# Row loads of the column scatters: asked for by GpSimd in the middle of each step, in place of SP's queue

## The chip, the core and the metric

The program runs on 1 core of one Trainium2 chip. Engines: PE is TensorE (matmuls), PEld its weight loads, DVE is VectorE, ACT is ScalarE, POOL is GpSimd, SP is SyncE, which here only asks for transfers. Each engine works through its own instructions in program order and waits for others by semaphores. The metric is the time of one execution in device microseconds; the median of three runs before the change is 14245.91 us (14245.34 to 14246.84).

## The reference, cut to what matters

The program is a tower of eight blocks on 128 images of 64 x 64. The first is a Fourier neural operator of four layers; then come attention and expert layers, and at the end a graph attention over 8192 nodes with 262144 listed edges and one loop per node, 270336 in all, followed by experts. What the change touches serves that graph block:

```python
loops = jnp.arange(M, dtype=edge_index.dtype)
src = jnp.concatenate([edge_index[0], loops])
dst = jnp.concatenate([edge_index[1], loops])
...
e_max = jax.ops.segment_max(e, dst, num_segments=M)
ee = jnp.exp(e - e_max[dst])
denom = jax.ops.segment_sum(ee, dst, num_segments=M)
...
agg = jax.ops.segment_sum(msg, dst, num_segments=M).reshape(M, HEADS * NUM_EXPERTS) + b_gat
```

The kernel computes these segment operations on edges sorted by `dst`. It sorts in two passes (a radix sort): first by the low 7 bits of the node ("column"), then by the rest ("row"). The first pass and the ranks of the second run beside the Fourier block.

## The kernel before, in words

`fno` is one stage between two barriers of all engines (`Tower.stage`, barriers at L59 and L65). It works through 16 units (4 groups of 32 images x 4 layers), each of 4 chunks of 8 images, so 64 chunks, numbered n = 0 to 63. In a chunk PE makes eight products `to_y` (L566), counted by the semaphore `y_done` (512 in all), each followed by the product with `f_proj` (L547) that is summed in a bank for `f_qa`. DVE adds that sum to `f_qa` once a chunk (L762, `q_added`), and the first L547 of the next chunk waits for that add. ACT moves and rectifies between the products. At the end of a unit comes the blend (L590), at the end of a group the head (L597), whose result `hq` is written out by `h_out` (L400, to `tower_h`); the first L652 of the next group waits until that has landed.

Beside it runs the column pass of the sort:

- DVE ranks the edges, a few columns per chunk (`rank_part`, before the chunk's L762). The 2112 columns of 128 edges are ranked in 4 parts of 528; `placed` counts parts that are ready.
- POOL scatters them: 48 steps of 44 columns, one indirect DMA per column (L2097), 128 rows of 8 bytes to `sorted1` at places `r_pos`. Step k begins when `y_done` has reached `send_at(k) + 1` (96 + 5.5 k, rounded down, plus 1) and its second half of 22 columns at `send_at(k) + 4`. The scatters of step k count on semaphore k mod 8 (`pool_column0` to `pool_column7`).
- Its source rows are loaded into one of two halves of `r_rows` by `rows(k)` (L375 to L378), 44 KB each. `rows(k)` waits until all scatters of step k - 2 have landed.
- At chunk 50 (`ROW_CHUNK`) the sorted list is read back: SP loads the `nodes` in four parts (L390) after `scattered`, DVE takes the row keys from them (L2091) and counts them (L2073) in chunks 50 to 52, and ranks them in the chunks from 53 on.

The order of SP's queue is written out in `sync` (L402 to L434): per unit the weights of the next (`f_stage`, L368), then chunk by chunk what is due there, then `projection_in` (`f_proj`, L373) and, after a group's last unit, `h_out`. `group_in` (L361 to L363) loads the next group's image, spectrum and features at chunk 2 of a group's last unit. `rows(k + 2)` stands at chunk (send_at(k) + 4) // 8.

Of the kernel before, what the change touches and what calls it, by code (L numbers as in the profile page):

```python
# [195 lines left out]
HD_SENDS = 8  # L196
# [111 lines left out]
def fno(t, d, ranks):  # L308
# [4 lines left out]
    send_at = lambda k: FIRST_SEND + 11 * k // 2  # L313
# [4 lines left out]
    with ExitStack() as ctx:  # L318
# [27 lines left out]
        with t.stage(*names) as (block, g_loaded, x0_done, x0_moved, x1_done, x1_moved, lift_done, lift_moved, q0_done, q0_moved,  # L346
                                 staged, wm_ready, proj_in, x_done, x_moved, t_done, t_moved, a_done, a_moved, y_done, r_done, used, q_added,
                                 f_moved, e_done, e_moved, w_done, spec_added, own, relu_done, o_done, o_moved, h_sent, rows_even, rows_odd, counted, summed, based, placed, place_out, scattered, nodes_in, nodes_used, row_placed, row_out, *sent):
            rows_in = (rows_even, rows_odd)
# [6 lines left out]
            @block.sync  # L356
            def _(sp):
                def group_in(gi):
                    if gi >= 1:
                        sp.wait_ge(a_done, 32 * LAYERS * gi)  # L360
                    sp.dma_start(xi, d["image_y"][gi].rearrange("y b x -> y (b x)")).then_inc(g_loaded, 16)  # L361
                    sp.dma_start(x16, d["grid_spectrum"]).then_inc(g_loaded, 16)
                    sp.dma_start(feat, d["features"][gi]).then_inc(g_loaded, 16)  # L363

                def weights_in(u):
                    if u >= 1:
                        sp.wait_ge(wm_ready, 6 * u)
                    sp.dma_start(stage[:].rearrange("p a b c e -> p (a b c e)"), f.folded[u % LAYERS]).then_inc(staged, 16)  # L368

                def projection_in(u):  # L370
                    if u >= 1:
                        sp.wait_ge(used, yi(u, 0, 0))
                    sp.dma_start(proj[:].rearrange("p c o y -> p (c o y)"), f.projections[u % LAYERS]).then_inc(proj_in, 16)  # L373

                def rows(k):  # L375
                    if k >= 2:
                        sp.wait_ge(sent[(k - 2) % HD_SENDS], 16 * STEP_COLS * ((k - 2) // HD_SENDS + 1))
                    sp.dma_start(ranks.rows[:, k % 2], ranks.edges[:, k * STEP_COLS:(k + 1) * STEP_COLS, :]).then_inc(rows_in[k % 2], 16)  # L378

                def place_part(part):  # L380
                    sp.wait_ge(placed, part + 1)
                    sp.dma_start(ranks.column_place[:, part * QC:(part + 1) * QC], ranks.pos[:, part]).then_inc(place_out, 16)

                def nodes(part):
                    if part == 0:
                        sp.wait_ge(scattered, 1)
                        sp.wait_ge(place_out, 16 * PARTS)
                    else:
                        sp.wait_ge(nodes_used, part)
                    sp.dma_start(ranks.nodes[:], ranks.by_column[:, part * QC:(part + 1) * QC, :]).then_inc(nodes_in, 16)  # L390

                def row_part(part):
                    sp.wait_ge(row_placed, part + 1)
                    if part == 0:
                        sp.dma_start(ranks.end, ranks.ends[0:1, :]).then_inc(row_out, 16)
                    sp.dma_start(ranks.row_place[:, part * QC:(part + 1) * QC], ranks.pos[:, part]).then_inc(row_out, 16)

                def h_out(gi):
                    sp.wait_ge(o_moved, 2 * (gi + 1))
                    sp.dma_start(f.h[:, gi * PAIRS:(gi + 1) * PAIRS, :], hq).then_inc(h_sent, 16)  # L400

                group_in(0)  # L402
                weights_in(0)
                projection_in(0)
                rows(0)
                rows(1)
                for u in range(UNITS):
                    if u + 1 < UNITS:
                        weights_in(u + 1)
                    for ch in range(CHUNKS):  # L410
                        n = u * CHUNKS + ch
                        if ch == 2 and last_of(u) and u + 1 < UNITS:
                            group_in(u // LAYERS + 1)
                        for k in range(SEND_STEPS - 2):
                            if (send_at(k) + 4) // 8 == n:
                                rows(k + 2)
                                if k % PART_STEPS == 1:
                                    place_part(k // PART_STEPS)
                        if n == ROW_CHUNK:
                            for part in range(PARTS):  # L420
                                nodes(part)
                        if n > ROW_CHUNK:
                            for part in range(PARTS):
                                if row_done_at(part) == n - 1:
                                    row_part(part)
                    if u + 1 < UNITS:
                        projection_in(u + 1)
                    if last_of(u):
                        h_out(u // LAYERS)
                sp.wait_ge(h_sent, 16 * IGROUPS)  # L430
                for part in range(PARTS):
                    if row_done_at(part) >= UNITS * CHUNKS - 1:
                        row_part(part)
                sp.wait_ge(row_out, 16 * (PARTS + 1))  # L434

            @block.gpsimd
            def _(p):
                for k in range(SEND_STEPS):
                    p.wait_ge(placed, k // PART_STEPS + 1)
                    p.wait_ge(rows_in[k % 2], 16 * (k // 2 + 1))  # L440
                    p.wait_ge(y_done, send_at(k) + 1)
                    ranks.send(p, k, 0, STEP_COLS // 2, sent[k % HD_SENDS])
                    p.wait_ge(y_done, send_at(k) + 4)
                    ranks.send(p, k, STEP_COLS // 2, STEP_COLS, sent[k % HD_SENDS])
                for j in range(HD_SENDS):
                    p.wait_ge(sent[j], 16 * STEP_COLS * SEND_STEPS // HD_SENDS)
                p.sem_inc(scattered, 1)
# [1572 lines left out]
PARTS = 4  # L2020
QC = COLS // PARTS
STEP_COLS = 44
PART_STEPS = QC // STEP_COLS
SEND_STEPS = PARTS * PART_STEPS
# [476 lines left out]
def rows(v):  # L2501

    return np.tile(v[None], (P, 1))
# [153 lines left out]
```

## Time and profile before

| | |
|---|---|
| median of the runs | 14245.91 us |
| profiled execution, its own time | 14248.64 us |
| its span | 14246.8 us |
| granted TensorE clock, mean | 0.716 |
| PE busy | 8506.4 us (60%) |
| DVE busy | 6583.8 us (46%) |
| ACT busy | 3350.6 us (24%) |
| POOL busy | 6318.2 us (44%) |
| scatters of L2097 | 2112, 2049.9 us, mean 971 ns |

The profile is of one execution, in microseconds from the span's start. "Busy" is the time in which an engine worked; waits are put down to what released the engine, by semaphore events, and "issue" is time for which the profile shows no releaser. A row of the SP timeline with "x3" merges three issues and the time between them. A time in brackets at the end of a row is the engine's idle time before it. The Fourier stage lies between about 144 and 5256 us.

### The profile page before, as it was taken

The numbers are of one execution on the slowest core, as the hardware profiler recorded it, in microseconds if no ns is written. First come the engines' busy times: TensorE is split into PE (matmuls) and PEld (weight loads), VectorE is DVE, ScalarE is ACT, GpSimd is POOL, SyncE is SP. The second block draws the span as 40 slices with busy tenths as digits, with TensorE's granted clock in tenths as the row PEclk, the third lists the DMA queues.
The fourth block names the chain that finished last, engine by engine and source line by source line (L and its number), as shares of the span: only waits on it lengthen the run. The fifth ranks groups of instructions, "written<-read, shape, count | busy, mean of one in ns | idle before, by whom it ended". The sixth has DMA issues, their size and how long they took to land. (4 is left out here: it accounts for less than half of the span.)

```text
span 14246.8 us, 157338 instructions
## 1 busy us (share of the span) xinstructions
PE 8506.4 (60%) x62435; PEld 5418.0 (38%) x62435; DVE 6583.8 (46%) x9074; ACT 3350.6 (24%) x5899; POOL 6318.2 (44%) x6565
## 2 busy tenths in 40 slices
PE   6997798588899967987777774749520000000006
PEld 4775575366667735652222222536310000000004
DVE  5778376200007862139999994452421111111123
ACT  2443343244344432222222221222100000000001
POOL 0005577767710002646666663000036666666640
PEclk8997888788989875559999996555555555555555
DMA  2000000000000000000000001000001111111100
GB/s 102 9 11 18 12 12 11 19 12 20 11 25 9 12 18 10 1 1 2 2 2 2 2 2 1 1 0 0 0 10 19 19 19 17 19 19 19 17 12 7
DMA packets 290069, 178.08 MB, mean 12 GB/s; under 512 B 226797, under 2 KB 274957, under 8 KB 284752
## 3 DMA queue, kind: packets, MB, share of 16 engines
q0 software_dynamic: 209952, 32.71, 3.9%
q1 hardware_dynamic: 79472, 136.16, 3.0%
q8 instruction: 480, 7.86, 0.2%
q14 instruction: 165, 1.35, 0.0%
HBM read 116.87 MB, written 51.56 MB: 12 GB/s over the span
## 5 line engine op out<-in xcount | busy, mean ns | idle before, releaser
L2010 POOL DMA_INDIRECT sorted<-by_row_rows,by_row_idx x2112 | 2031.1, 962 | 2650.9 <-PE bank L1219 1729.1
L2097 POOL DMA_INDIRECT sorted<-r_rows,r_pos x2112 | 2049.9, 971 | 1926.3 <-PE bank L566 1284.5
L2229 POOL DMA_INDIRECT g_g<-table,g_idx x2112 | 2024.7, 959 | 643.6 <-issue 643.6
L1722 DVE TENSOR_TENSOR a_top<-bank,a_k 128x2048 f32<-128x2048 f32 x1024 | 2254.0, 2278 | 6.3 <-ACT a_k L1758 3.8
L2331 PE MATMUL bank<-sc_ident,g_tails 128*20 128x128 f32 x99 | 18.2, 307 | 3136.7 <-PEq L65 3134.9
L1884 PE MATMUL bank<-a_top,sc_pick_row 128*32 128x512 f32 x8192 | 1105.0, 620 | 515.5 <-DVE a_top L1722 492.6
L2331 PEld LDWEIGHTS bank<-sc_ident,g_tails 128*20 128x20 f32 x99 | 7.1, 98 | 3147.6 <-issue 3135.0
L2250 DVE CAST g_nodef<-g_es 128x64 f32<-128x64 int32 x33 | 6.4, 195 | 2492.9 <-DMA g_ep<-sorted 2492.9
L762 DVE TENSOR_TENSOR f_qa<-f_qa,bank 128x512 f32<-128x512 f32 x128 | 82.2, 684 | 2318.6 <-PE bank L556 1982.7
L547 PE MATMUL bank<-f_space,f_proj 128*128 128x512 f32 x2048 | 978.5, 601 | 199.7 <-issue 160.5
L1219 PEld LDWEIGHTS bank<-sw_e_w,e_hid 128*128 128x128 f32 (+1 forms) x4608 | 893.1, 329 | 363.6 <-issue 293.4
L2086 DVE TENSOR_TENSOR_SCAN r_run<-r_hit,r_base 128x528 f32<-128x528 bf16 x772 | 1017.3, 1318 | 27.6
L2227 POOL DMA_INDIRECT g_g<-table,g_first x33 | 31.1, 941 | 2139.2 <-DVEq L57 1741.8
L566 PE MATMUL bank<-f_space,f_to_y 96*128 96x512 f32 x2048 | 966.5, 599 | 19.1 <-ACT f_space L666 19.1
L1219 PE MATMUL bank<-sw_e_w,e_hid 128*128 128x64 f32 (+1 forms) x4608 | 933.9, 421 | 2.2 <-DVE e_part L1334 2.2
L681 ACT ACTIVATE f_space<-bank,f_b1r 128x512 f32<-128x512 f32 x1024 | 647.5, 683 | 832.8 <-PE bank L566 832.8
L556 PEld LDWEIGHTS bank<-f_from_y,f_space 128*128 128x128 f32 x6144 | 750.1, 193 | 185.4 <-issue 185.4
L556 PE MATMUL bank<-f_from_y,f_space 128*128 128x96 f32 x6144 | 741.0, 274 | 0.0
L1334 DVE TENSOR_TENSOR e_part<-bank,e_gates 128x512 f32<-128x512 f32 (+1 forms) x288 | 161.9, 571 | 1243.5 <-PE bank L1219 1243.4
L506 PE MATMUL bank<-f_space,f_spec 32*32 32x128 f32 x18432 | 521.9, 338 | 276.7 <-ACT f_space L652 211.7
L547 PEld LDWEIGHTS bank<-f_space,f_proj 128*128 128x128 f32 x2048 | 388.2, 192 | 675.2 <-issue 639.3
L1884 PEld LDWEIGHTS bank<-a_top,sc_pick_row 128*32 128x32 f32 x8192 | 166.8, 109 | 1228.1 <-DVE a_top L1722 1184.0
(467 smaller groups left out, 13013.8 us busy)
## 6 DMA issues: line engine op xcount, KB each, us to landing
f_stage<-folded SPq DMA_DIRECT2D x16, 2304.0 KB
sorted<-r_rows,r_pos POOLq DMA_INDIRECT x2112, 2.1
sorted<-by_row_rows,by_row_idx POOLq DMA_INDIRECT x2112, 2.1
g_g<-table,g_idx POOLq DMA_INDIRECT x2112, 2.6
states<-g_st SPq DMA_DIRECT2D x33, 768.0 KB
fp_raw<-t_modes SPq DMA_DIRECT2D x4, 2304.0 KB, 15.0
folded<-fp_turned SPq DMA_DIRECT2D x4, 2304.0 KB, 7.8
f_bb<-t_features SPq DMA_DIRECT2D x4, 2048.0 KB, 11.4
```

The source lines that it names most:

```text
L506: last = pe.matmul(out, spec[rows, kg, kx, r, :], rhs, start=(r == 0), stop=(r == 1), skip_group_check=True)
L547: last = pe.matmul(t.bank[4 + hf][:, :], proj[:, cg].rearrange("p o y -> p (o y)"), rr[:, cg % 2 * 2 + hf, :], start=(cg == 0), stop=(cg = ...
L556: last = pe.matmul(t.bank[6 + cg % 2][:, b * 96:(b + 1) * 96], rr[:, cg % 2 * 2 + hf, b * P:(b + 1) * P], const["from_y"][:, hf * 96:(hf + ...
L566: last = pe.matmul(t.bank[cg % 2 * 2 + hf][:, :], const["to_y"][:, hf * P:(hf + 1) * P], aa[:, cg, :], start=True, stop=True)
L681: last = act.activation(rr[:, cg % 2 * 2 + hf, :], t.bank[cg % 2 * 2 + hf][:, :], ACT.Relu, bias=f.b1r[:, u % LAYERS, cg:cg + 1])
L1219: last = pe.matmul(y_of(n, q)[:, col:col + D], hid[r, (2 * n + a) % HR, k * P:(k + 1) * P], w2[r, 2 * s + a, :], start=(j == 0), stop=(j = ...
L1722: v.tensor_tensor(top[:, n % RD].rearrange("p q (h s) -> p q h s", s=S), q, kk, ALU.max).then_inc(top_done, 1)
L1884: last = pe.matmul(sums[k % 2][32 * q:32 * q + 32, :], t.pick_row[:, i, :], top[:, n % RD, q, :], start=False, stop=(i == I16 - 1), skip_g ...
L2010: p.indirect_dma_start(out=self.dst, out_offset=bass.IndirectOffsetOnAxis(ap=self.idx[:, k:k + 1], axis=0), in_=self.rows[:, k, :], in_off ...
L2086: c.link(v.tensor_tensor_scan(self.run[:], self.hit[:], self.hit[:], self.base[:, i:i + 1], ALU.add, ALU.bypass))
L2097: p.indirect_dma_start(out=self.dst, out_offset=bass.IndirectOffsetOnAxis(ap=self.pos[:, k // PART_STEPS, at:at + 1], axis=0), in_=self.ro ...
L2229: p.indirect_dma_start(out=g[:, k_in, j, :], out_offset=None, in_=d["table"], in_offset=bass.IndirectOffsetOnAxis(ap=idx[:, k_in, j:j + 1] ...
```

## The change

The row loads leave SP's queue and are asked for by POOL. `rows(0)` stands at the start of POOL's part of the stage; `rows(k + 1)` stands in the middle of step k, between its two halves of 22 scatters, and waits for the scatters of step k - 1. `place_part` stays in SP at the same chunks. Nothing else changes.

```diff
--- before.py
+++ after.py
@@ -372,11 +372,6 @@
                         sp.wait_ge(used, yi(u, 0, 0))
                     sp.dma_start(proj[:].rearrange("p c o y -> p (c o y)"), f.projections[u % LAYERS]).then_inc(proj_in, 16)
 
-                def rows(k):
-                    if k >= 2:
-                        sp.wait_ge(sent[(k - 2) % HD_SENDS], 16 * STEP_COLS * ((k - 2) // HD_SENDS + 1))
-                    sp.dma_start(ranks.rows[:, k % 2], ranks.edges[:, k * STEP_COLS:(k + 1) * STEP_COLS, :]).then_inc(rows_in[k % 2], 16)
-
                 def place_part(part):
                     sp.wait_ge(placed, part + 1)
                     sp.dma_start(ranks.column_place[:, part * QC:(part + 1) * QC], ranks.pos[:, part]).then_inc(place_out, 16)
@@ -402,8 +397,6 @@
                 group_in(0)
                 weights_in(0)
                 projection_in(0)
-                rows(0)
-                rows(1)
                 for u in range(UNITS):
                     if u + 1 < UNITS:
                         weights_in(u + 1)
@@ -411,11 +404,9 @@
                         n = u * CHUNKS + ch
                         if ch == 2 and last_of(u) and u + 1 < UNITS:
                             group_in(u // LAYERS + 1)
-                        for k in range(SEND_STEPS - 2):
-                            if (send_at(k) + 4) // 8 == n:
-                                rows(k + 2)
-                                if k % PART_STEPS == 1:
-                                    place_part(k // PART_STEPS)
+                        for part in range(PARTS):
+                            if (send_at(PART_STEPS * part + 1) + 4) // 8 == n:
+                                place_part(part)
                         if n == ROW_CHUNK:
                             for part in range(PARTS):
                                 nodes(part)
@@ -435,11 +426,19 @@
 
             @block.gpsimd
             def _(p):
+                def rows(k):
+                    if k >= 2:
+                        p.wait_ge(sent[(k - 2) % HD_SENDS], 16 * STEP_COLS * ((k - 2) // HD_SENDS + 1))
+                    p.dma_start(ranks.rows[:, k % 2], ranks.edges[:, k * STEP_COLS:(k + 1) * STEP_COLS, :]).then_inc(rows_in[k % 2], 16)
+
+                rows(0)
                 for k in range(SEND_STEPS):
                     p.wait_ge(placed, k // PART_STEPS + 1)
                     p.wait_ge(rows_in[k % 2], 16 * (k // 2 + 1))
                     p.wait_ge(y_done, send_at(k) + 1)
                     ranks.send(p, k, 0, STEP_COLS // 2, sent[k % HD_SENDS])
+                    if k + 1 < SEND_STEPS:
+                        rows(k + 1)
                     p.wait_ge(y_done, send_at(k) + 4)
                     ranks.send(p, k, STEP_COLS // 2, STEP_COLS, sent[k % HD_SENDS])
                 for j in range(HD_SENDS):
```

In SP's queue around the end of the first group (unit 3), before. `f_bb` is a group's image and features, `f_stage` the next unit's weights, `pool_column`n the semaphores of the scatters, `used` and `wm_ready` PE's and ACT's progress:

```order
L368 DMA f_stage<-folded 128x4608 [waits wm_ready]
L378 DMA r_rows<-listed 128x88 [waits pool_column0]
L378 DMA r_rows<-listed 128x88 [waits pool_column1]
L382 DMA place<-r_pos 128x528 [waits placed]
L378 DMA r_rows<-listed 128x88 [waits pool_column2]
L361 DMA f_bb<-t_image_y 64x2048 [waits a_done]
L362 DMA f_space<-t_grid_spectrum 16x4608
L363 DMA f_bb<-t_features 128x4096
L378 DMA r_rows<-listed 128x88 [waits pool_column3]
L378 DMA r_rows<-listed 128x88 [waits pool_column4]
L378 DMA r_rows<-listed 128x88 [waits pool_column5]
L373 DMA f_proj<-projections 128x1024 [waits used]
```

The same place in SP's queue now (line numbers have moved: `h_out`, L400 before, is L395):

```order
L368 DMA f_stage<-folded 128x4608 [waits wm_ready]
L377 DMA place<-r_pos 128x528 [waits placed]
L361 DMA f_bb<-t_image_y 64x2048 [waits a_done]
L362 DMA f_space<-t_grid_spectrum 16x4608
L363 DMA f_bb<-t_features 128x4096
L373 DMA f_proj<-projections 128x1024 [waits used]
L395 DMA tower_h<-f_space 128x1024 [waits o_moved]
```

Six row loads, each with a wait for scatters, no longer stand between the weights' load and the projection's.

POOL's queue from the stage's start, before:

```order
L2097 DMA sorted<-r_rows,r_pos 270336x2 [waits y_done,rows_even,placed]
L2097 DMA sorted<-r_rows,r_pos 270336x2 x21
L2097 DMA sorted<-r_rows,r_pos 270336x2 [waits y_done]
L2097 DMA sorted<-r_rows,r_pos 270336x2 x21
L2097 DMA sorted<-r_rows,r_pos 270336x2 [waits y_done,rows_odd,placed]
```

The same place now (L2096 is the scatter, L432 the row load):

```order
L432 DMA r_rows<-listed 128x88
L2096 DMA sorted<-r_rows,r_pos 270336x2 [waits y_done,rows_even,placed]
L2096 DMA sorted<-r_rows,r_pos 270336x2 x21
L432 DMA r_rows<-listed 128x88
L2096 DMA sorted<-r_rows,r_pos 270336x2 [waits y_done]
L2096 DMA sorted<-r_rows,r_pos 270336x2 x21
L2096 DMA sorted<-r_rows,r_pos 270336x2 [waits y_done,rows_odd,placed]
L2096 DMA sorted<-r_rows,r_pos 270336x2 x21
L432 DMA r_rows<-listed 128x88 [waits pool_column0]
L2096 DMA sorted<-r_rows,r_pos 270336x2 [waits y_done]
```

One row load stands between the two halves of each step, and from the second step on it waits for the scatters of the step before.

## Rows read from the trace of the kernel before

**Rows 1.** The page, busy tenths of the span in 40 slices, TensorE and GpSimd.
```profile
PE   6997798588899967987777774749520000000006
...
POOL 0005577767710002646666663000036666666640
```

**Rows 2.** Timeline of PE: start us, length us, operation, [idle before].
```profile
5293.77 3.63 PE L826 MATMUL bank<-sc_ident,a_x 128*64 128x128 f32 x16 [48.42 <-PEq L65]
```

**Rows 3.** Waits of SP, 0 to 4200: releaser, total us, times, longest.
```profile
SPq L378 <- DMA sorted<-r_rows,r_pos: 2735.2, 46, 126.2
```

**Rows 4.** Timeline of the SP queue, 1300 to 4100.
```profile
1323.27 0.47 SPq L361 DMA_DIRECT2D f_bb<-t_image_y  x1
...
1379.88 111.61 SPq L378 DMA_DIRECT2D r_rows<-listed  x3
1491.54 0.43 SPq L373 DMA_DIRECT2D f_proj<-projections  x1
1492.01 0.43 SPq L400 DMA_DIRECT2D tower_h<-f_space  x1
...
2191.81 0.43 SPq L373 DMA_DIRECT2D f_proj<-projections  x1
...
4003.61 0.33 SPq L373 DMA_DIRECT2D f_proj<-projections  x1
...
4081.91 0.32 SPq L368 DMA_DIRECT2D f_stage<-folded  x1
```

**Rows 5.** Waits of PE, 1100 to 5300.
```profile
PE bank L506 <- ACT f_space L652: 211.7, 2, 106.5
PE bank L547 <- issue: 160.5, 5, 50.4
...
PE bank L456 <- DMA f_bb<-t_features: 32.4, 2, 19.1
```

**Rows 6.** Waits of ACT, 1100 to 5300.
```profile
ACT f_space L652 <- DMA tower_h<-f_space: 214.1, 2, 107.7
```

**Rows 7.** Timeline of PE at two of its stalls.
```profile
1498.31 5.36 PE L506 MATMUL bank<-f_space,f_spec 32*32 32x128 f32 x144 [106.50 <-ACT f_space L652]
...
2195.58 3.75 PE L547 MATMUL bank<-f_space,f_proj 128*128 128x512 f32 x4 [50.41 <-issue]
```

**Rows 8.** Line L373 (loads of f_proj): issue to landing.
```profile
DMA to landing us min/median/max: 3.4/3.7/17.2
```

**Rows 9.** Timeline of DVE: adds to f_qa and the first row key.
```profile
2237.14 1.28 DVE L762 TENSOR_TENSOR f_qa<-f_qa,bank 128x512 f32<-128x512 f32 x2 [79.61 <-PE bank L556]
...
4242.60 0.43 DVE L2091 TENSOR_SCALAR r_run<-r_nodes 128x528 int32<-128x528 int32 x1
...
4307.19 1.29 DVE L762 TENSOR_TENSOR f_qa<-f_qa,bank 128x512 f32<-128x512 f32 x2
...
4357.51 1.29 DVE L762 TENSOR_TENSOR f_qa<-f_qa,bank 128x512 f32<-128x512 f32 x2
```

**Rows 10.** Timeline of POOL: its two waits between first and last scatter.
```profile
1566.43 0.96 POOL L2097 DMA_INDIRECT sorted<-r_rows,r_pos  x1 [76.42 <-PE bank L566]
...
2949.46 0.95 POOL L2097 DMA_INDIRECT sorted<-r_rows,r_pos  x1 [56.46 <-PE bank L566]
```

**Rows 11.** Line L2097 (scatters): duration ns, first and last start us, landing.
```profile
L2097 POOL DMA_INDIRECT sorted<-r_rows,r_pos x2112: 952/958/1654, 1150.9 to 3975.7; - x192
...
DMA to landing us min/median/max: 2.1/2.1/6.5
```

**Rows 12.** Line L378 (row loads in SP): issue ns min/median/max.
```profile
L378 SPq DMA_DIRECT2D r_rows<-listed x48: 319/320/433, 146.8 to 3866.8; - x48
```

**Rows 13.** Line L390 (loads of the nodes): issue to landing.
```profile
DMA to landing us min/median/max: 3.6/3.9/10.6
```

**Rows 14.** Groups of POOL in 3000 to 3900 and in 2250 to 2500.
```profile
L2097 POOL DMA_INDIRECT sorted<-r_rows,r_pos x713 | 682.7, 957 | 217.4 <-issue 216.5 <-PE bank L566 0.9
...
L2097 POOL DMA_INDIRECT sorted<-r_rows,r_pos x194 | 191.5, 987 | 59.1 <-issue 59.1
```

## The prediction, made before the changed kernel ran

> **What bounds the kernel now.** I began with the busy slices [rows 1]. GpSimd (POOL) works in slices 4 to 12, the Fourier stage of the program, where TensorE (PE) is at eight or nine tenths in most slices but falls to seven and five in some. So PE sets this stage's pace and is held up somewhere. After the stage all engines meet at a barrier: PE's first work behind it waits for L65, the barrier's line [rows 2]. A microsecond saved ahead of the barrier is therefore a microsecond of the whole, and the question is only what ends this stage.
>
> SP's own waits come next [rows 3]. The row loads of L378 waited 2735.2 us on earlier scatters, in 46 instalments of up to 126.2 us. SP is one queue in program order, so all that stands behind such a wait is late too. The SP timeline shows which transfers those are [rows 4]: the image of the next group at 1323.27, which stood behind a row load that had just come free; `f_proj` at 1491.54 and `tower_h` at 1492.01, straight behind three row loads spread over 111.61 us; `f_proj` again at 2191.81, and so at three later places. Where no row load stands ahead (4003.61), `f_proj` goes out by itself.
>
> Does anybody wait for these? ACT waited 214.1 us in two places for `tower_h` to land [rows 6], and of PE's waits [rows 5] 211.7 us are for what ACT wrote then (L652), 160.5 us in 5 places stand at L547 and are put down to "issue", and 32.4 us in 2 places are for `f_bb<-t_features`. L547 is the product with `f_proj`: at 2195.58 PE has stood idle for 50.41 us and starts 3.8 us after SP's issue of 2191.81 [rows 7, 4], which is the landing time of `f_proj` (median 3.7 us) [rows 8]. These three rows are PE time lost to SP's row loads: 211.7 + 160.5 + 32.4 = 404.6 us, all before chunk 50, where the sorted list is first read.
>
> **What the change does to it, term by term.** SP loses 48 transfers and their 46 waits. `place_part` stays, but waits for a part that VectorE (DVE) has long finished. The loads that PE and ACT missed then go out when their own condition is met, as at 4003.61. I count the whole 404.6 us as gone from PE's chain up to chunk 50. DVE should not take PE's place there: its ranking is the same, and it waited 79.61 us for PE before the add at 2237.14 [rows 9]; with PE 50.41 us sooner [rows 7] some 29 us of wait are left.
>
> DVE begins the row keys of chunk 50 at 4242.60 [rows 9], right behind the add of chunk 49, for which it waits on PE. By PE alone that would become 4242.6 - 404.6 = 3838.0.
>
> But the row keys also need the scatters finished. POOL runs from 1150.9 to 3976.7 (last start 3975.7 and 0.96 for it) [rows 11]. In between it waited twice for PE's L566, 76.42 and 56.46 us [rows 10]. Both come behind stalls of PE that go: at 1566.43 PE is at least the 106.50 us of 1498.31 [rows 7] sooner, at 2949.46 more. So 132.9 us go, and the 2112 scatters end at 3976.7 - 132.9 = 3843.8, about the earliest possible, since nothing but 0.30 us stands between one scatter and the next.
>
> Into this chain the change puts 47 row loads (the 48th, `rows(0)`, is at the stage's start, where POOL is idle until 1150.9). No plain DMA asked for by POOL is in this trace. The near rows: SP's issue of the same load takes 0.320 us [rows 12], POOL's scatter 0.958 us, at most 1.654 us [rows 11], each plus 0.30 us between. Low end: 0.62 us each, 29 us. High end: 1.95 us each, 92 us. I take POOL's own scatter, also 128 partitions with a small piece each: 0.97 + 0.30 = 1.27 us, and 47 x 1.27 = 60 us. The new wait of each load, for the scatters of the step before, costs nothing: they were asked for at least 22 x 1.27 = 28 us earlier and land in 2.1 us, at most 6.5 [rows 11]. What is queued behind the load on POOL is 22 scatters, so the rows have the same 28 us to land before POOL asks for them.
>
> POOL then ends at 3843.8 + 59.7 = 3903.5. The last scatter lands (2.1 us); SP, which by then stands at `nodes(0)`, since the `f_stage` load ahead of it (4081.91 before [rows 4]) is past by 3677, issues (0.32) and the nodes land (3.9 [rows 13]): 3903.5 + 6.3 = 3909.8. That is 72 us later than PE would allow, so POOL becomes the bound, and the row keys start 4242.6 - 3909.8 = 332.8 us sooner than before.
>
> The rest of the unit shifts by the same. From the first row key to the add of chunk 50 DVE needs 64.6 us (4242.60 to 4307.19), and to that of chunk 51 another 50.3 us (4357.51), with no wait for PE ahead of either [rows 9]. PE, now ahead, stops at its first L547 of chunk 51 until the add of chunk 50 is done and is held by DVE to the unit's end, so its next work also starts 333 us sooner. From there all is as before.
>
> Sum against the profiled execution: 14248.64 - 332.8 = 13915.8. The median of the runs, 14245.91, lies 2.7 below that execution, which gives **13913 us**, 2.3% less.
>
> **Two pages of the Trainium skill against the rows.** Its page "DMA: Bandwidth & Descriptors", section "Issuing engines are not separate DMA queues", says that spreading DMAs over issuing engines saves only the time of issuing them, usually small. By that rule 48 x 0.32 us of SP would be all that is saved, and no time. The trace speaks against it here, since what SP's queue holds back is not the issuing but the waits in front of it (2735.2 us [rows 3]); its result is the second rival. The page "SBUF — State Buffer", section "SBUF: two separate sides", warns that a DMA issued from GpSimd stands still while VectorE holds the port that the two share, and gives some 620 ns alone against some 3100 ns beside such a copy. By it, 47 loads at 3.1 + 0.3 us would be an estimated 160 us. The rows show little of it: the same scatter takes a mean of 957 ns while DVE hardly works (3000 to 3900) and 987 ns while it ranks (2250 to 2500) [rows 14].
>
> **Rivals.** First, a dear row load. If POOL spends over 2 us on each plain load, the gain shrinks by 47 us for each microsecond. Against it: the 2112 scatters on this engine all stay under 1.66 us. For it: no such load is in the trace. At 4 us each: 3843.8 + 188 + 6.3 = 4038, a gain of 204.5 us, 14041 us.
>
> Second, no change. If PE's 160.5 us at L547, named only as "issue", and ACT's 214.1 us had other causes than SP's order, PE would still reach chunk 50 at 4242. POOL's 60 us would lie inside its 4242.6 - (3976.7 + 6.3) = 260 us of slack there, and the time is 14246. Against it: the stall ends 3.8 us behind SP's issue.
>
> Third, slower. One mechanism: POOL's chain grows past the point at which chunk 50 waited for PE. It decides from (4242.6 - 3843.8 - 6.3) / 47 = 8.35 us per load on, be it by issue or because the rows land so late in POOL's own queue, behind 22 scatters, that POOL waits for them (landing after 28 + 7 us). At 10 us each the row keys start at 4320, 77 us late: 14323 us. Against it: scatters land in 2.1 us at the median, so the queue is not backed up.
>
> **How the numbers follow.** Forecast (loads of 0.6 to 2 us, POOL the new bound) 0.80, dear load 0.12, no change 0.03, slower 0.05. Within the first the ends are 13913 - 31 = 13882 and 13913 + 32 = 13945. The range goes up to 13990, a load of 2.9 us, and starts at 13878. The runs shown differ by 0.01%; 0.2% (28 us) is taken as what a measurement tells from no change. Faster by that needs a load under 7.8 us: 0.92; same 0.03; slower 0.05.
>
> **What would show it.** In the profile of the changed kernel: no wait of SP for scatters; ACT without the 214.1 us for `tower_h`; L547 without idle times of 30 to 50 us; POOL without idle time for L566 after its first scatter, its last scatter near 3903; 48 plain loads on POOL of about 1 us; and as a new wait some 72 us of DVE's row keys for `r_nodes`, with PE held at L547 of chunk 51. It would be wrong if the last scatter came before 3870 or after 3950, if POOL waited for its rows, if DVE held PE in chunks 16 to 31, or if the stage ended earlier by another figure than POOL's.

## The result

The changed kernel takes 13885.71 us (median of 4 runs, 13873.11 to 13896.99) against 14246.38 us before (4 runs): a ratio of 0.9746, 95% interval 0.9729 to 0.9763. The forecast was 13913 (range 13878 to 13990). The profiled execution took 13896.99 us, its span is 13895.2 us.

SP's waits in the profile after, the line that answers [rows 3] being gone (columns: releaser, total us, times, longest):

```profile
SPq L373 <- PE bank L555: 2047.3, 9, 269.8
SPq L361 <- PE bank L529: 512.2, 3, 171.7
...
SPq L395 <- ACT f_space L700: 265.9, 4, 192.1
SPq L385 <- POOLq L446: 202.6, 1, 202.6
```

No row load waits for scatters in SP's queue any more. The one wait of SP for POOL that is left is that of the nodes (L385) for the end of all scatters: SP stood there for 202.6 us before POOL was through. Every load now waits for its own condition only, as the SP timeline shows (against [rows 4]): `f_bb` goes out at 1254.37 in place of 1323.27 and `tower_h` (now L395) at 1323.96 in place of 1492.01.

```profile
1254.37 0.47 SPq L361 DMA_DIRECT2D f_bb<-t_image_y  x1
...
1323.96 0.33 SPq L395 DMA_DIRECT2D tower_h<-f_space  x1
...
3885.09 15.18 SPq L385 DMA_DIRECT2D r_nodes<-sorted  x4
```

PE's waits (against [rows 5]: 211.7, 160.5 and 32.4 us, all gone), and what stands there now:

```profile
PE bank L546 <- DVE f_qa L761: 84.1, 5, 45.2
...
PE bank L596 <- ACT f_qa L697: 61.2, 4, 30.1
```

ACT has no wait for `tower_h` any more ([rows 6] had 214.1 us). POOL's waits in the same stretch: none of the two of [rows 10], only the 1005.6 us ahead of the first scatter and 1.5 us in five places, each of them the 0.30 us that stand between any two scatters.

```profile
POOL sorted L2096 <- PE bank L565: 1007.1, 6, 1005.6
POOL sorted L2096 <- issue: 642.0, 2106, 0.3
```

POOL's scatters and its row loads by line (duration ns min/median/max, first and last start; against [rows 11, 12]):

```profile
L2096 POOL DMA_INDIRECT sorted<-r_rows,r_pos x2112: 954/958/1937, 1151.2 to 3882.8; - x192
```

```profile
L432 POOL DMA_DIRECT2D r_rows<-listed x48: 570/582/704, 144.9 to 3799.9; - x48
```

The last scatter ends at 3882.8 + 0.96 = 3883.8. SP asks for the nodes at 3885.09 and DVE's first row key starts at 3888.76 (against 4242.60 in [rows 9]), after a wait that was not there before:

```profile
3888.76 0.43 DVE L2090 TENSOR_SCALAR r_run<-r_nodes 128x528 int32<-128x528 int32 x1 [47.58 <-DMA r_nodes<-sorted]
...
3894.34 0.44 DVE L2090 TENSOR_SCALAR r_run<-r_nodes 128x528 int32<-128x528 int32 x1 [4.68 <-DMA r_nodes<-sorted]
```

PE, ahead by then, is held at the first L546 of chunk 51, as forecast, and the stage ends (PE's first work behind the barrier, against 5293.77 in [rows 2]) at 4940.15:

```profile
3955.25 3.75 PE L546 MATMUL bank<-f_space,f_proj 128*128 128x512 f32 x4 [45.21 <-DVE f_qa L761]
```

```profile
4940.15 3.63 PE L825 MATMUL bank<-sc_ident,a_x 128*64 128x128 f32 x16 [48.26 <-PEq L65]
```

So the row keys start 353.8 us sooner, the stage ends 353.6 us sooner, and the profiled execution is 351.65 us shorter (14248.64 - 13896.99); 2.0 us are given back behind the stage.

The four runs lie in two pairs, 13896.99 and 13894.48, 13876.94 and 13873.11. The profile is of the upper pair. That is why the medians differ by 360.7 us and the profiled executions by 351.7; what sets the two pairs apart was not profiled.

### The profile page after: what moved, and what is told of

Same layout as the page of the kernel before. It is cut to its first block and busy times, and to the rows that moved or that the text cites. A ratio compares the mean times of both kernels' runs of the same rounds, so it can differ in the third digit from the quotient of the medians.

```text
span 13895.2 us, 157338 instructions
## 1 busy us (share of the span) xinstructions
PE 8501.9 (61%) x62435; PEld 5412.3 (39%) x62435; DVE 6583.5 (47%) x9074; ACT 3354.1 (24%) x5899; POOL 6357.6 (46%) x6613
## 5 line engine op out<-in xcount | busy, mean ns | idle before, releaser
L2096 POOL DMA_INDIRECT sorted<-r_rows,r_pos x2112 | 2061.8, 976 | 1649.0 <-PE bank L565 1007.1
L2085 DVE TENSOR_TENSOR_SCAN r_run<-r_hit,r_base 128x528 f32<-128x528 bf16 x772 | 1017.4, 1318 | 27.6
L546 PE MATMUL bank<-f_space,f_proj 128*128 128x512 f32 x2048 | 971.6, 597 | 86.5 <-DVE f_qa L761 84.1
L546 PEld LDWEIGHTS bank<-f_space,f_proj 128*128 128x128 f32 x2048 | 386.0, 191 | 559.2 <-issue 521.3
L1203 PE MATMUL bank<-e_xt,sw_e_w 64*128 64x512 f32 x1024 | 527.5, 1129 | 113.3 <-ACT e_hid L1281 113.3
```

The source lines that it names most:

```text
L546: last = pe.matmul(t.bank[4 + hf][:, :], proj[:, cg].rearrange("p o y -> p (o y)"), rr[:, cg % 2 * 2 + hf, :], start=(cg == 0), stop=(cg = ...
L1203: pe.matmul(h_bank[(2 * n + a) % 4][:, :], w1[r, s, :], xt[r, g * 512:(g + 1) * 512], start=True, stop=True).then_inc(u_done, 1)
L2085: c.link(v.tensor_tensor_scan(self.run[:], self.hit[:], self.hit[:], self.base[:, i:i + 1], ALU.add, ALU.bypass))
L2096: p.indirect_dma_start(out=self.dst, out_offset=bass.IndirectOffsetOnAxis(ap=self.pos[:, k // PART_STEPS, at:at + 1], axis=0), in_=self.ro ...
```

## The experiments

Twelve runs of five kernels. They fell into two conditions of the chips that have to be told apart. In the first the kernel before takes 14246 to 14267 us, as in the result above; `early` and `half3` ran so, each with one execution of the kernel and one of the kernel before, so that they are read by what their profiles show and not by an interval. In the second the kernel before takes 16898 to 17056 us, and every kernel of this study came within 0.4% of it; the other ten ran so, on chips 1, 4, 6, 9 and 10 (`load_late3`, `load_late4` and `load_twice2` with one execution each). The chip is not the cause by itself: chip 4 showed the kernel before at 16997 with `half2` and at 14257 with `early`. What brings the second condition about is open.

### again: the changed kernel once more

No edit.

> The changed kernel once more. Theory: POOL's chain is the bound, so the spread of its runs (13873 to 13897) is the spread of POOL's scatters: in this profile the time less the start of the row keys (3888.8 in the first profile) stays within 3 us of 13897.0 - 3888.8 = 10008, whatever the time is. Rival: the spread comes from a later stage; then the row keys start at 3889 within 3 us in any run and the rest differs. Expected 13886 within 12.

Measured: 17022.52 us against 17021.66 before, ratio 1.0001 (0.9992 to 1.0009). The question on the spread of the changed kernel was not answered, but the run shows the second condition. Busy time by stretch (columns: stretch, its length, then PE, PEld, DVE, ACT, POOL busy with counts, granted clock, DMA share, GB/s), ahead of the first scatter, beside the scatters, and behind the last (5407):

```profile
0.00:1150.00 1150.00, 1000.35 (x9273) 741.26 (x9274) 797.95 (x1276) 442.26 (x768) 0.91 (x5) 0.90 0.11 40
2000.00:3000.00 1000.00, 634.11 (x4915) 452.72 (x4915) 409.63 (x659) 239.88 (x421) 483.44 (x504) 0.74 0.04 8
5500.00:6000.00 500.00, 468.07 (x4421) 345.81 (x4420) 173.40 (x158) 217.98 (x375) 0.00 (x0) 0.87 0.07 22
```

and the changed kernel in the first condition:

```profile
2000.00:3000.00 1000.00, 946.19 (x7942) 683.22 (x7931) 346.88 (x558) 436.31 (x746) 763.98 (x792) 0.91 0.07 15
```

Where POOL does not scatter, PE is 87% (0 to 1150) and 94% busy (5500 to 6000). Beside the scatters it is 63% busy, with 95% in the first condition. The granted clock falls there too, 0.74 in place of 0.91, but that is the smaller part: a matmul takes PE 8% longer (634.11 us for 4915 in place of 946.19 us for 7942), while it stands idle for 366 us in place of 54. The waits say why. ACT's in 1150 to 5410, DVE's in 1150 to 2000, and one such moment on the timelines of PE, ACT and DVE:

```profile
ACT f_space L671 <- remote: 1202.0, 80, 39.4
ACT f_space L665 <- remote: 479.6, 36, 43.6
```

```profile
DVE r_hit L2084 <- remote: 29.8, 15, 2.0
DVE r_run L2085 <- DVE r_hit L2084: 18.0, 19, 1.1
```

```profile
1219.39 2.02 PE L529 MATMUL bank<-f_to_x,f_bb 96*96 96x128 f32 x8 [32.46 <-issue]
1241.79 2.02 PE L529 MATMUL bank<-f_to_x,f_bb 96*96 96x128 f32 x8 [20.38 <-issue]
```

```profile
1241.14 0.59 ACT L665 ACTIVATE f_space<-bank 96x512 f32<-96x512 f32 x1 [21.81 <-remote]
```

```profile
1241.14 0.51 DVE L2084 TENSOR_SCALAR r_hit<-r_key,sc_iota 128x528 bf16<-128x528 bf16 x1 [1.99 <-remote]
```

"remote" is a release for which no engine of the core is found. DVE waits 1.0 us for its own instruction before (L2085 for L2084, 19 times up to 2000), a wait that does not show at all in the first condition. PE's products of 1219.39 are done at 1221.41, ACT takes them up only at 1241.14, and PE's next ones start 0.65 us after that. For 19.7 us neither of the two works. I read this as semaphore signals that arrive late while the scatters run. They seem to arrive in batches: the 13 late starts of DVE between 1214 and 1249 us lie at whole multiples of 0.70 us from each other, and twice, at 1218.74 and at 1241.14, ACT starts in the same instant as DVE. Such waits for a "remote" release are seen in the two stretches with scatters and hardly outside them (none before 1150, 13.6 us of ACT between 5410 and 7070). The gathers of the graph block, issued just as densely, take the same time in both (10155.0 to 13252.7 in the profile after, 13244.6 to 16368.6 here, 3098 and 3124 us), though no other engine hands POOL work there, so they test little; but the second scatter pass, beside experts and attention, takes 4294 us in place of 3105. Where POOL scatters and other engines hand work to each other, it costs. In this condition POOL waits for PE between its scatters as well (1713.1 us in all, 1009.3 of them ahead of the first scatter; 1007.1 and 1005.6 in the first condition), and the row keys start at 5762.84, 356 us after the last scatter: the stage is bound by PE, and POOL's chain has slack.

### load_twice and load_twice2: what one row load costs POOL

```diff
+ self.spare = sb("spare", [P, 2, STEP_COLS, 2], I32)
...
  p.dma_start(ranks.rows[:, k % 2], ...).then_inc(rows_in[k % 2], 16)
+ spare_in = (spare_even, spare_odd)[k % 2]
+ if k >= 2:
+     p.wait_ge(spare_in, 16 * (k // 2))
+ p.dma_start(ranks.spare[:, k % 2], ...).then_inc(spare_in, 16)
```

> Each row load is asked for twice by POOL, the second copy into a spare tile that nobody reads. Theory (POOL is the bound, a load costs it 0.6 to 0.9 us with what it does to the scatter behind it): 48 more loads move POOL's end and the total by 27 to 41 us, to about 13920. Rival (PE or DVE sets the start of the row keys, POOL has slack): no change, 13886. Rival (a dear load, 2 us or more): 13980 or more.

Measured: 16986.96 against 17021.66 (second condition), ratio 0.9984 (0.9975 to 0.9993). POOL has slack here, so neither the theory nor the rival was put to the test.

> As load_twice: a second copy of each row load, into a spare tile. A load costs POOL 0.58 us and 0.30 behind it, and a scatter behind it is slower by up to 0.75 us while DVE works. Theory (POOL is the bound): one more load per step adds 0.58 to 0.88 us each, 27 to 41 us: last scatter 3910 to 3924, row keys 3916 to 3930, total near 13920. Rival (POOL has slack): row keys 3889, no change.

Measured: 17026.71 against 17056.45, the second condition again, so the total says nothing of the theory. The price of a load can still be read off POOL's timeline, which here shows the load, the second load and the scatter behind:

```profile
1315.11 0.58 POOL L432 DMA_DIRECT2D r_rows<-listed  x1
1315.69 0.57 POOL L436 DMA_DIRECT2D r_spare<-listed  x1
1316.57 0.99 POOL L2103 DMA_INDIRECT sorted<-r_rows,r_pos  x1 [0.30 <-issue]
```

The second load starts 0.58 us after the first, with nothing in between, and the 0.30 us that stand between scatters come once. A load adds 0.58 us to POOL's queue, not 0.58 + 0.30. In the first condition the profile after has the same 0.58 (median 582 ns). That twice as many loads would cost 27 us where POOL is the bound was not seen as a total.

### load_late to load_late4: what the middle of the step is worth

```diff
  ranks.send(p, k, 0, STEP_COLS // 2, sent[k % HD_SENDS])
- if k + 1 < SEND_STEPS:
-     rows(k + 1)
  p.wait_ge(y_done, send_at(k) + 4)
  ranks.send(p, k, STEP_COLS // 2, STEP_COLS, sent[k % HD_SENDS])
+ if k + 1 < SEND_STEPS:
+     rows(k + 1)
```

> The row load stands at the end of each step, right ahead of the scatters that need it, in place of the middle. Theory: the 22 scatters behind a load in the middle cover its landing; without them POOL waits for the landing at each of 47 steps, some 1.5 to 2.2 us, 70 to 105 us in all: 13955 to 13990. Rival (the landing is not covered by anything anyway, or it is much longer, since the load queues behind 44 scatters): no change, 13886, or over 14030.

Measured: 16976.24 against 17021.66, ratio 0.9973 (0.9961 to 0.9985).

> As load_late: the row load at the end of each step, right ahead of the scatters that need it. Where the kernel before takes about 14246 us: theory (22 scatters in between cover the landing) POOL waits 1.5 to 2.2 us at each of 47 steps, 13955 to 13990 in all; rival (nothing to cover, or a much longer landing behind 44 scatters) 13886 or over 14030.

Measured: 16945.49 against 16997.46, ratio 0.9969 (0.9960 to 0.9979).

> As load_late: the row load at the end of each step, right ahead of the scatters that need it. Where the kernel before takes about 14250 us: theory (22 scatters in between cover the landing) POOL waits 1.5 to 2.2 us for r_rows at each of 47 steps, the last scatter near 3965 and the total 70 to 105 us over the changed kernel, 13955 to 13990; rival (nothing to cover) last scatter 3883, 13886.

Measured: 17010.63 against 17056.45.

> The row load at the end of each step once more, by itself. Each load then has 2.2 us between it and the next scatter, where the changed kernel has 0.30 (seen in load_late2 and load_late3). Where the kernel before takes about 14250 us: POOL is the bound, so 47 x 1.9 = 89 us come on top of the changed kernel's POOL chain: last scatter near 3972, row keys 3978, total 13960 to 13990. Rival (POOL is not the bound): row keys 3889, 13886.

Measured: 16851.7 against 16898.43. All four in the second condition, where POOL has slack, and none could show the total that was forecast. What the timeline of load_late3 does show is the gap behind the load:

```profile
1287.98 0.58 POOL L432 DMA_DIRECT2D r_rows<-listed  x1
1290.85 0.99 POOL L2096 DMA_INDIRECT sorted<-r_rows,r_pos  x1 [2.29 <-issue]
```

2.29 us pass between load and scatter where the load stands right ahead of its use, 0.30 us in the changed kernel; the shortest of the 47 gaps here is 2.20 us. The landing costs about 2.0 us more than it takes to pass on, and 22 scatters (28 us) cover it easily. 47 x 2.0 = 94 us would be the price where POOL is the bound; that total was not seen. That this kernel is 0.3% faster than the kernel before here, in all four runs, is measured twice with an interval and not explained: with PE as the bound, a POOL that pauses between steps may leave the signals more room, but no run separates that.

### half, half2 and half3: are the stalls a sum, or does SP tie PE to POOL?

POOL asks for the rows of steps 0 to 23, as in the changed kernel; SP asks for those of steps 24 to 47 at their old places, with the old waits and two semaphores of their own (the numbering of lines moves by 14 behind them).

```diff
  def rows(k):                      # in SP
+     if k < 24:
+         return
...
+ def rows(k): ...                  # in POOL, as in the changed kernel
+ if k + 1 < 24:
+     rows(k + 1)
```

> The row loads of steps 0 to 23 by POOL as in the changed kernel, those of steps 24 to 47 by SP at their old places. Theory A: the stalls are not a sum, SP's last row waits tie PE to POOL's steps; from step 24 on PE falls back to POOL's pace, and only POOL's own lead counts: its wait of 76.4 us at 1566 goes, 23 loads cost 19, so 57 us gained, 14189 (row keys at 4185), with one stall of PE near unit 7 of some 190 us. Theory B: each stall is lost for itself, so those ahead of chunk 28 (106.5 + 13.2 + 50.4 + 48.4 = 218 us) go and the later ones stay: 14028.

Measured: 17008.61 against 17021.66, ratio 0.9995 (0.9986 to 1.0004).

> As half, on another chip if it comes so: row loads of steps 0 to 23 by POOL, of steps 24 to 47 by SP at their old places. Where the kernel before takes about 14246 us: theory A (SP's last row waits tie PE to POOL's steps, stalls don't add up) 14189 with the row keys at 4185; theory B (each stall is lost for itself) 14028. Where it takes about 17020 us, as in the run before, handshakes between engines are late while POOL scatters, and nothing of either is seen.

Measured: 16992.1 against 16997.46, ratio 0.9999 (0.9990 to 1.0009). It shows at work why the change gains nothing in the second condition. From the SP timeline, the part with SP's row loads at their old places:

```profile
4752.96 443.29 SPq L380 DMA_DIRECT2D r_rows<-listed  x6
5230.43 0.32 SPq L373 DMA_DIRECT2D f_proj<-projections  x1
```

The six row loads are through at 4752.96 + 443.29 = 5196.3, and `f_proj` goes out 34 us later, when PE lets it. There are four more such places. At three of them `f_proj` goes out 0.8 to 65 us after the last row load; at the fourth (3624.82) it goes straight behind, but PE is then still busy with the head's products. At none of the five does a wait of PE end with its landing. With PE behind POOL, SP's row waits are over before anything behind them is needed.

> As half: row loads of steps 0 to 23 by POOL, of steps 24 to 47 by SP at their old places. Where the kernel before takes about 14250 us: theory A (SP's last row waits tie PE to POOL's steps, stalls don't add up) 14189 with the row keys at 4185 and one PE stall near unit 7 of some 190 us; theory B (each stall is lost for itself) 14028.

Measured, in the first condition: 14203.89 against 14266.9 on the same chip, one execution each (14189 and 14028 were the two theories). PE's stalls in 1100 to 5300, and the row keys (the lines are those of this kernel: L560 is the product with `f_proj`, L2104 the row keys):

```profile
PE bank L560 <- issue: 232.8, 3, 174.6
PE bank L519 <- ACT f_space L665: 104.7, 2, 104.5
```

```profile
2479.40 0.32 SPq L380 DMA_DIRECT2D r_rows<-listed  x1
2479.77 0.43 SPq L373 DMA_DIRECT2D f_proj<-projections  x1
```

```profile
2483.76 3.63 PE L560 MATMUL bank<-f_space,f_proj 128*128 128x512 f32 x4 [174.56 <-issue]
```

```profile
4191.20 0.43 DVE L2104 TENSOR_SCALAR r_run<-r_nodes 128x528 int32<-128x528 int32 x1
```

```profile
2897.03 0.96 POOL L2110 DMA_INDIRECT sorted<-r_rows,r_pos  x1 [55.14 <-PE bank L579]
```

SP's first row load, that of step 24, goes out at 2479.40 after 525.1 us of waiting for scatters; `f_proj`, queued behind it, follows at 2479.77, and PE starts 4.0 us later. This one stall of 174.56 us at unit 7 holds almost all that was saved ahead of it (190 was expected), the later stalls are back nearly as before, and the row keys start at 4191.20, 51.4 us sooner than before (57 expected). Theory B, a sum, would have given some 218. POOL's first wait of [rows 10] is gone and its second is there with 55.14 us. This shows that SP's row waits tie PE to POOL's steps: PE's stalls in the kernel before are one debt, paid wherever SP's queue next holds something that PE needs. Freeing the first half of the stretch did not free PE; freeing all of it up to chunk 50 did. Other splits were not run.

### early and early2: POOL starts a chunk sooner

```diff
- FIRST_SEND = 12 * 8
+ FIRST_SEND = 11 * 8
```

> The changed kernel with FIRST_SEND = 11 * 8 in place of 12 * 8, so that POOL's first scatter waits for the ranks of part 0 (about 1049) and not for chunk 12 (1151), and all later conditions are 8 products sooner. Nothing else. Theory (POOL's chain sets the start of the row keys, PE would allow them at 3841): POOL is 86 us ahead from chunk 12 on and ends near 3797, the row keys start at 3841 right behind DVE's add, without a wait for the first r_nodes, and 47 us are gained on the changed kernel: about 13840. Rival (PE is slowed by earlier scatters, or DVE bounds): row keys at 3889, 13886. Where the kernel before takes about 17020 us, PE does not lead POOL and the time stays within 0.3% of it.

Measured, in the first condition: 13830.21 against 14257.29 on the same chip, one execution each (13840 expected). The row keys and the scatters:

```profile
3846.20 1.29 DVE L761 TENSOR_TENSOR f_qa<-f_qa,bank 128x512 f32<-128x512 f32 x2 [52.89 <-PE bank L555]
3847.41 0.43 DVE L2090 TENSOR_SCALAR r_run<-r_nodes 128x528 int32<-128x528 int32 x1
```

```profile
L2096 POOL DMA_INDIRECT sorted<-r_rows,r_pos x2112: 954/958/1914, 1050.2 to 3801.2; - x192
```

POOL's last scatter starts at 3801.2 (3797 was the expected end) and the first row key stands right behind DVE's add, without a wait: PE is the bound again. Against the changed kernel (3888.76) the row keys are 41.4 us sooner, where 47 were expected, since PE itself comes 6.3 us later: DVE's add ahead of the row keys starts at 3846.20 and not at 3839.89 as in the changed kernel. The stage ends at 4896.33, 43.8 us sooner. This takes one suspected bound away and the time follows: in the changed kernel POOL's chain was the bound. DVE waited 47.58 us for it there, and 41.4 of these are gained.

The span is 66.8 us shorter than that of the changed kernel, so 23 us come from behind the stage. They lie in the first block behind the barrier, attention and experts. Two stretches of 100 us there, from 260 us behind the barrier on, in `early` and then in the changed kernel:

```profile
5156.00:5256.00 100.00, 96.37 (x405) 68.40 (x405) 17.06 (x40) 24.70 (x41) 75.92 (x80) 0.60 0.02 1
5256.00:5356.00 100.00, 96.37 (x349) 68.85 (x349) 21.58 (x41) 21.66 (x36) 63.24 (x66) 0.50 0.02 1
```

```profile
5200.00:5300.00 100.00, 96.37 (x348) 68.66 (x349) 14.84 (x35) 20.93 (x34) 61.45 (x65) 0.50 0.02 1
5300.00:5400.00 100.00, 96.37 (x348) 68.12 (x344) 21.99 (x43) 20.93 (x34) 63.50 (x65) 0.50 0.02 1
```

In `early` the granted clock of the first of the two is 0.60, in the changed kernel 0.50, the lower of the two levels (1.2 GHz of 2.4); in the same 100 us PE gets through 405 matmuls in place of 348. In the 260 us ahead of them it is 0.54 against 0.52, with 618 matmuls in place of 592, PE being busy for 167 us of them in both. At the lower level the 57 + 26 = 83 more would have taken 83 / 348 x 100 = 24 us, an estimate, and the whole block is 24 us shorter (1041.3 against 1065.5 us from the barrier). So of `early`'s 66.8 us some 23 go with the clock. The code is the same there; whether the edit brings the higher clock about, or it comes in some executions of either kernel, one profile of each cannot tell. The two pairs of the changed kernel's runs lie 20 us apart, and this may be the same difference.

> The version with FIRST_SEND = 11 * 8 timed against the kernel before: row keys at 3847 as in early, 13830 to 13855 against 14246 to 14267, a ratio of 0.970 to 0.973; the changed kernel had 0.9746. Where the kernel before takes about 17020 us: a ratio between 0.99 and 1.00, as every kernel had there.

Measured: 17016.78 against 16990.8 in the second condition, ratio 1.0013 (1.0003 to 1.0022); the row keys start at 5781.11, 463 us behind the last scatter. The expected ratio, 0.99 to 1.00, was just missed. A head start of POOL is worth nothing where PE is the bound. So `early` beats both kernels by one execution in the first condition (13830.21; its stage 43.8 us shorter than the changed kernel's), and none of the kernels gains over 0.4% in the second.

## Why the prediction was right

**PE's 404.6 us.** Right. All three waits are gone; without POOL the row keys could have started at 3888.76 - 47.58 = 3841.2, forecast 3838.0. The prediction added the stalls up as if each were lost for itself. The sum holds only because every row load up to chunk 50 left SP's queue: with half of them left there, `half3` gained 51.4 us and not some 218.

**POOL becomes the bound.** Right, and shown by `early`: with POOL's head start the row keys move by 41 us and the wait for `r_nodes` goes. The wait was 47.6 us in place of 72, since the row keys could start 21 us sooner by POOL and 3 us later by PE than thought.

**POOL's two waits of 132.9 us.** Right, both gone: 1.5 us in five places are left.

**47 x 1.27 = 60 us for the row loads.** Too dear; this is the mis-sized term. POOL's chain grew from 3843.8 to 3883.8, by 40 us. A load takes 0.58 us and follows the scatter ahead of it without a gap (load_twice2), 47 x 0.58 = 27 us. The scatter behind it is slower: 1.73 us in ten of the first 22 steps, about 1.3 in four, and 0.98 in all steps after 2400, DVE's ranking of the columns being at its end (2429). That is 10 x 0.75 + 4 x 0.33 = 9 us. The argument against a dear load, that all scatters stay under 1.66 us, held for the kernel before; in the changed one the longest took 1.94 us. Some scatters elsewhere in the steps are slower too: all 2112 together were busy for 2061.8 us in place of 2049.9, and 27.3 + 11.9 = 39.2 us of the 40. Each of the ten scatters of 1.73 us ends 0.05 to 0.07 us before the end of an L2087 of DVE that it overlaps, as here, and the 0.75 us more are about the length of that instruction:

```profile
1180.72 1.73 POOL L2096 DMA_INDIRECT sorted<-r_rows,r_pos  x1 [0.30 <-issue]
```

```profile
1181.76 0.74 DVE L2087 COPY_PREDICATED r_posf<-r_hit,r_run 128x528 f32<-128x528 uint16 x1
```

Most scatters that overlap an L2087 take no longer for it, so this is a coincidence in time and not a cause shown. Between the ends of the range (29 and 92 us) the value lay near the low one, SP's own issue.

**From POOL's end to the row keys.** 5.0 us in place of 6.3. With 19.7 us at POOL's end that is the whole difference of 21.0 us between 332.8 and 353.8.

**The two rules of the Trainium skill.** "Issuing engines are not separate DMA queues" (DMA: Bandwidth & Descriptors) would have given no change. No run here puts a price on the issuing itself; what the change took away was waiting in program order, 2735.2 us of it. The warning of the Trainium skill's "SBUF: two separate sides" (SBUF — State Buffer) fits in kind and not in size: beside DVE the scatter behind a plain load took 1.73 us in place of 0.98, 9 us in all and not the estimated 100 more.

**The rest of the unit and of the program.** Right: 353.8 at the row keys, 353.6 at the barrier, 351.7 at the end. The median came out 27 us under the forecast. Of these 18.9 are the 21.0 us above less the 2.0 that were given back behind the stage; the other 8.6 come from the median lying 11.3 us under the profiled execution, where the forecast took over 2.7 from the kernel before. Nothing in the prediction speaks of that, and it brought the median to 8 us from the lower end of the range.

**The rivals.** A dear load: refuted by 0.58 us. No change: refuted in the first condition by the waits that are gone and by the ratio of 0.9746; but it is exactly what happens in the second, for a reason that no rival named: PE is slowed beside the scatters until it no longer leads POOL. Slower: refuted, POOL never waited for its rows, and `load_late3`, in the second condition, puts their landing at about 2.3 us behind the load, against 28 us of cover.

## What to carry to other kernels

A queue that only asks for transfers is still a queue: when one of its entries waits for a slow chain, everything behind it is tied to that chain, and the idle times of the other engines are one debt. Here moving half of the entries only put it off to the next place. Put the request into the queue of the engine whose progress it waits for, far enough ahead of its use that the landing is covered. Then ask what is late next: here it was that engine's own chain, by 47.6 us, and an earlier start took it off the path and gained 41.4 of them, in one execution.

## What was not expected of the hardware

- The same program takes 13886 us in one condition and 17022 us in another. DVE, ACT and POOL are busy for the same time in both (6583.5 and 6600.7, 3354.1 and 3336.9, 6357.6 and 6345.8 us), PE for 8% more (8501.9 and 9205.2) at a lower granted clock (0.720 and 0.669); the rest is idle time. As read above, signals between engines arrive late there, seen almost only while POOL scatters to HBM (20.38 us between two products of PE, 1.0 us for DVE to see its own). The gain of 2.5% is none there. What brings it about is open.
- A plain load asked for by POOL takes it 0.58 us, less than an indirect one of the same number of partitions (0.96), and no gap stands ahead of it. While DVE ranks, the scatter behind it can take 1.73 us in place of 0.98.
- The clock that PE is granted over the same 100 us behind the barrier differed between two kernels that are the same there, 0.60 and 0.50; with the 260 us ahead (0.54 and 0.52) it goes with 24 us.
